# Second attention of a fused two-layer kernel: batch 1's high keys are copied by ScalarE instead of GpSimd, and three key pieces of batch 2 are split later

## The chip, the cores and the metric

The kernel is one program on 1 core of a Trainium2 chip. The metric is device time in microseconds (us) for one execution, the median of several. The engines are TensorE (PE; its weight loads are PEld), VectorE (DVE), ScalarE (ACT), GpSimd (POOL) and SyncE (SP), which issues most DMA transfers. Each engine runs its own instructions in order, and semaphores hold it back where it needs another engine's result.

## The reference, cut to what matters

Two layers of cross-attention and expert feed-forward are applied to `x` of shape 8 x 256 x 256 (batch, rows, features), with a context `ctx_2048` of 8 x 1601 x 256. The change touches the attention of the second layer, in which the context is key and value at once:

```python
def _L1_xattn_ref(hidden_states, memory_tokens, memory_mask):
    scores = jnp.einsum('bsd,bmd->bsm', hidden_states, memory_tokens) * scale      # scale = 256 ** -0.5
    scores = jnp.where(memory_mask[:, None, :], scores, neg_inf)
    attn = jax.nn.softmax(scores, axis=-1)
    readout = jnp.einsum('bsm,bmd->bsd', attn, memory_tokens)
    return jnp.where(valid_b[:, None, None], readout, 0)
...
x = x + _L0_xattn_ref(_layernorm(x), ctx_2048, ...)
x = x + _L0_ffn_ref(_layernorm(x), ...)
x = x + _L1_xattn_ref(_layernorm(x), ctx_2048, mask_BxS2_bk0)
x = x + _L1_ffn_ref(_layernorm(x), ...)
```

Everything is float32 in the reference. The kernel gets that accuracy from TensorE by splitting each operand into a high part (a copy rounded to the type `fp32r`) and a low part (original minus high), and adding three products: high x high, high x low, low x high.

## The kernel before

The program runs its stages one after the other: projections, the first attention (most of the time), the first feed-forward (`moe_two_of_eight`), the second attention (`memory_attention`), routing (`route_to_slots`) and the second feed-forward (`moe_slots`). `memory_attention` runs from 2519 us to about 2700 us of the span.

**Units.** `x` is 16 tiles of 128 rows, two to a batch. `memory_attention` works one tile at a time; a tile is a unit, and `body(i, last)` does four units u = 0 to 3, which are two batches, for i = 0 to 3. The 13 blocks of 128 keys of a batch are cut into four pieces, `MEM_PIECES`: pieces 0 to 2 have three blocks (128x768 elements, two features per partition and key) and piece 3 has four (128x1024). For a unit n and piece p:

- TensorE computes the scores into `ps_s` (`scores`, six matmuls in `score_piece`, L1426 to L1428); VectorE adds the mask's penalty and takes the piece's maximum (`piece_maximum`, L2215), then the row's (`negative_maximum`, L2222).
- ScalarE takes the exponential (`exp`, L2124); TensorE transposes the probabilities into `ps_t` (`transposes`, L2342); ScalarE copies them as high part (`high`, L2133) and VectorE subtracts for the low part (`low`, L2240).
- TensorE multiplies them with the context's rows (`products`, L2359 to L2361). VectorE forms the inverse of the row sum (`inverse_sum`, L2226 to L2231) and adds to `x` (`add_x`, L2248).

A later unit's normalised rows are made by GpSimd (`normalise`, L2074; VectorE's own for tiles 2 and 3, L2191), transposed (`transpose_x`, L2323), and split by `high_x` (ScalarE, L2139) and `low_x` (VectorE, L2198).

**Order of the work.** It is written out by hand, the same slots s = 0 to 3 on each engine. On TensorE slot s of unit u holds: the transposes of two pieces ahead, the products of piece s, in slot 2 `transpose_x` of unit u + 3, then the scores of unit u + 2, piece s. So the scores of unit 2, the first of batch 1, are made in the four slots of unit 0, and those of unit 4, the first of batch 2, in unit 2.

**Keys and rows.** The context is loaded twice for each batch, as transposed keys (`load_keys`, L1401) and as rows (`load_rows`, L1406), each into one raw buffer without a second copy (`area`, keys half and rows half). A piece of the next batch is loaded by SyncE once the present one has been split. For keys: `t_hi` (ScalarE, `split_t`, L2109) and `t_lo` (GpSimd, `split_t`, L2060); for rows: `r_hi` (ScalarE, `split_r`, L2116) and `r_lo` (GpSimd, `split_r`, L2068). The keys of even batches go to `keys_even`, those of odd ones to `keys_odd`. Batch 0's keys are split in the stage before. What is special at the start of this stage:

- Batch 1's high keys are four copies by GpSimd (L2079), its low keys four subtractions by VectorE (`low_t`, L2253): piece 0 ahead of unit 0, pieces 1 to 3 in slots 1 to 3 of unit 0. The scores of unit 2 wait for each (`wait_low`).
- Batch 0's rows: high parts by ScalarE (three ahead of the exponentials of unit 0, the fourth behind `high_x`); low parts 0 and 1 by VectorE (`low_r`, L2259), 2 and 3 by GpSimd.
- Batch 2's keys: high and low parts of piece 0 in slot 0 of unit 0, piece 1 in slot 2 of unit 0, pieces 2 and 3 in unit 1. Batch 1's rows lie between them, in the odd slots on ScalarE.

SyncE loads in the order batch 2's keys piece x, batch 1's rows piece x, for x = 0 to 3; each keys load waits for `low_t` of that piece.

## Time and profile before

| | |
|---|---|
| median of 3 runs | 2907.09 us (2905.89 to 2907.46) |
| the profiled execution | 2901.44 us |
| its span (first to last instruction) | 2899.6 us |
| busy share of the span: PE, PEld, DVE, ACT, POOL | 96%, 84%, 71%, 68%, 59% |
| mean granted TensorE clock | 0.979 of full speed |
| opening of the second attention, TensorE's first score of it to the first product of unit 0 | 2519.1 to 2529.1 us of the span |
| units 0, 1, 2, 3 by TensorE | 15.4, 10.8, 11.8, 10.8 us |

Times in the rows are microseconds from the span's start. A busy share says how long an engine worked, not whether anyone waited for it; for a change that moves a few instructions within 40 us, the rows of those 40 us count. A matmul's recorded duration contains its drain, so consecutive matmuls overlap and their pitch is shorter than their duration; other engines' instructions overlap by about 0.1 us in the same way. "[1.81 <-DVE pt_lo L2240]" behind a row says that the engine was idle for 1.81 us ahead of it and that VectorE's `pt_lo` ended the wait.

### The profile page before, as it was taken

Reading aid. Unit: us, or ns where it says so; the run is one execution under the profiler, and the core shown is the slowest. Engines: PE = TensorE matmul, PEld = TensorE weight load, DVE = VectorE, ACT = ScalarE, POOL = GpSimd, SP = SyncE. Lnnn points to the kernel's source line nnn. Section 1 sums busy time; section 2 is a strip of 40 time slices with the busy share of each in tenths; the row PEclk is TensorE's granted clock in tenths of the full one; section 3 lists DMA queues with packets and bytes.
Section 4 is the critical chain, followed back from the end, with each engine's and each line's share of the span. In section 5 each row is a group of like instructions: output and inputs, shape, how many; then the busy total and the mean of one; then the engine's idle time right before and its main releaser. Section 6 shows DMA issues by size and latency. Waiting matters only on the chain. (4 is left out here: it accounts for less than half of the span.)

```text
span 2899.6 us, 57707 instructions
## 1 busy us (share of the span) xinstructions
PE 2774.8 (96%) x18157; PEld 2441.3 (84%) x18157; DVE 2056.7 (71%) x4859; ACT 1968.1 (68%) x4913; POOL 1711.9 (59%) x2139
## 2 busy tenths in 40 slices
PE   7989999799999999999999999999999998799698
PEld 5768888699999999999999999999999985599655
DVE  7985445577777777777777777777777778965444
ACT  5656666577777777777777777777777756766111
POOL 6766663366665665666666566666656537587122
PEclk9999999899999999999999999999999998999699
DMA  5447667611111211111111111111111016364510
GB/s 184 133 143 217 205 206 209 211 43 71 50 50 44 70 57 43 71 53 47 46 68 57 43 71 56 44 48 66 57 43 71 15 37 145 80 198 132 191 36 27
DMA packets 284603, 263.46 MB, mean 91 GB/s; under 512 B 46382, under 2 KB 260527, under 8 KB 284304
## 3 DMA queue, kind: packets, MB, share of 16 engines
q1 hardware_dynamic: 264784, 238.94, 25.9%
q10 hardware_dynamic: 17312, 15.73, 1.9%
q0 software_dynamic: 2208, 5.12, 0.6%
q8 instruction: 148, 2.42, 0.4%
q14 instruction: 151, 1.24, 0.1%
HBM read 167.34 MB, written 84.93 MB: 87 GB/s over the span
## 5 line engine op out<-in xcount | busy, mean ns | idle before, releaser
L1031 ACT ACTIVATE w_hi<-ps_t 128x512 fp32r<-128x512 f32 (+2 forms) x1024 | 568.5, 555 | 352.6 <-PE ps_t L1274 344.3
L1133 DVE TENSOR_TENSOR w_lo<-ps_t,w_hi 128x512 fp32r<-128x512 f32 (+2 forms) x1024 | 655.8, 640 | 178.6 <-ACT w_hi L1031 175.3
L1107 DVE TENSOR_REDUCE piece_max<-ps_s 128x1 f32<-128x512 f32 (+1 forms) x768 | 472.3, 622 | 238.3 <-PE ps_s L1261 221.8
L1294 PE MATMUL ps_o<-w_hi,v_hi 128*128 128x256 f32 (+1 forms) x1856 | 596.0, 321 | 0.0
L1204 POOL TENSOR_SCALAR prob<-prob,inv_sum 128x512 f32<-128x512 f32 (+2 forms) x768 | 478.2, 642 | 189.6 <-DVE inv_sum L1123 189.6
L1296 PE MATMUL ps_o<-w_hi,v_lo 128*128 128x256 f32 (+1 forms) x1856 | 523.5, 282 | 0.0
L1295 PE MATMUL ps_o<-w_lo,v_hi 128*128 128x256 f32 (+1 forms) x1856 | 522.2, 281 | 0.0
L1274 PE MATMUL ps_t<-ident,prob 128*128 128x128 f32 (+1 forms) x2784 | 517.7, 273 | 0.0
L1274 PEld LDWEIGHTS ps_t<-ident,prob 128*128 128x128 f32 (+1 forms) x2784 | 357.1, 140 | 62.7 <-DVE w_lo L1133 8.7
L1259 PE MATMUL ps_s<-k_hi,q_hi 128*128 128x512 f32 (+2 forms) x1024 | 395.8, 387 | 10.2 <-PEq L58 4.8
L1260 PE MATMUL ps_s<-k_lo,q_hi 128*128 128x512 f32 (+2 forms) x1024 | 377.5, 369 | 0.0
L1261 PE MATMUL ps_s<-k_hi,q_lo 128*128 128x512 f32 (+2 forms) x1024 | 375.9, 367 | 0.0
L1019 ACT ACTIVATE prob<-ps_s,neg_max 128x512 f32<-128x512 f32 (+1 forms) x576 | 366.9, 637 | 0.0
L1295 PEld LDWEIGHTS ps_o<-w_lo,v_hi 128*128 128x128 f32 (+1 forms) x1856 | 353.7, 191 | 0.0
L1294 PEld LDWEIGHTS ps_o<-w_hi,v_hi 128*128 128x128 f32 (+1 forms) x1856 | 352.3, 190 | 0.0
L1296 PEld LDWEIGHTS ps_o<-w_hi,v_lo 128*128 128x128 f32 (+1 forms) x1856 | 350.0, 189 | 0.0
L1219 POOL TENSOR_TENSOR v_lo<-raw_v,v_hi 128x512 fp32r<-128x512 f32 x124 | 149.6, 1217 | 191.4 <-ACT v_hi L1047 191.4
L1274 PE MATMUL ps_t<-ident,first_prob 128*128 128x128 f32 (+1 forms) x928 | 230.1, 272 | 1.4 <-DVE w_lo L1133 1.2
L1212 POOL TENSOR_TENSOR k_lo<-raw_k,k_hi 128x480 fp32r<-128x480 f32 x124 | 148.9, 1222 | 138.8 <-ACT k_hi L1040 138.8
L1259 PEld LDWEIGHTS ps_s<-k_hi,q_hi 128*128 128x128 f32 x1024 | 194.9, 190 | 35.7 <-ACT prob L1019 18.2
L1261 PEld LDWEIGHTS ps_s<-k_hi,q_lo 128*128 128x128 f32 x1024 | 194.2, 190 | 28.1
L1260 PEld LDWEIGHTS ps_s<-k_lo,q_hi 128*128 128x128 f32 x1024 | 195.9, 191 | 2.9
(318 smaller groups left out, 6358.6 us busy)
## 6 DMA issues: line engine op xcount, KB each, us to landing
v_scratch<-v_out SPq DMA_DIRECT2D x120, 256.0 KB, 3.0
raw_k<-k_scratch SPq DMA_DIRECT2D x32, 960.0 KB, 7.0
raw_v<-v_scratch SPq DMA_DIRECT2D x32, 960.0 KB, 4.7
k_scratch<-k_out SPq DMA_DIRECT2D x104, 256.0 KB, 2.7
q_scratch<-out_t SPq DMA_DIRECT2D x64, 256.0 KB, 2.5
r_all<-r_scratch SPq DMA_DIRECT2D x32, 512.0 KB, 4.2
raw_q<-q_scratch SPq DMA_DIRECT2D x32, 512.0 KB, 5.1
first_prob<-in_ctx_t ACTq DMA_DIRECT2D x50, 256.0 KB, 2.8
```

What stands on the lines that cost most here:

```text
L1019: nc.scalar.activation(prob[n % PB][:, lo:hi], source, ACT.Exp, bias=neg_max[:, n % PB:n % PB + 1], accum_out=piece_sum[:, n % 2, p:p + 1] ...
L1031: nc.scalar.activation(pt_hi[keys, k % RING, cols], ps_t[keys, k % 2, cols], ACT.Copy).then_inc(hi_done, 1)
L1107: nc.vector.tensor_reduce(piece_max[:, n % 2, p:p + 1], ps_s[:, p, lo - p * PC:hi - p * PC], AX.X, ALU.max).then_inc(max_ready, 1)
L1133: nc.vector.tensor_tensor(pt_lo[keys, k % RING, cols], ps_t[keys, k % 2, cols], pt_hi[keys, k % RING, cols].bitcast(F32), ALU.subtract).th ...
L1204: nc.gpsimd.tensor_scalar(prob[n % PB][:, lo:hi], prob[n % PB][:, lo:hi], inv_sum[:, n % PB:n % PB + 1], 1.0, ALU.mult, ALU.mult).then_inc ...
L1259: nc.tensor.matmul(out, q_hi[gi][:, h, qs], k_hi[gi][:, lo:hi], start=True, stop=False)
L1260: nc.tensor.matmul(out, q_hi[gi][:, h, qs], k_lo[gi][:, lo:hi], start=False, stop=False)
L1261: nc.tensor.matmul(out, q_lo[gi][:, h, qs], k_hi[gi][:, lo:hi], start=False, stop=True).then_inc(scores_ready, 1)
L1274: last = nc.tensor.transpose(ps_t[0:keys, k % 2, at:at + P], prob[(2 * u + j) % PB][:, blk * P:blk * P + keys], ident[:, :])
L1294: nc.tensor.matmul(out, v_hi[gi][keys, vs], pt_hi[keys, k % RING, cols], start=blk == (0 if qt else 1), stop=False)
L1295: nc.tensor.matmul(out, v_hi[gi][keys, vs], pt_lo[keys, k % RING, cols], start=False, stop=False)
L1296: last = nc.tensor.matmul(out, v_lo[gi][keys, vs], pt_hi[keys, k % RING, cols], start=False, stop=blk == KB - 1)
```

## The change

In the opening, ScalarE copies batch 1's high keys (`first_t`), each behind the high part of the same piece of rows; GpSimd's four copies are gone. Two of batch 0's row pieces (1 and 2) are split after exponentials instead of ahead of them. In unit 0 only piece 0 of batch 2's keys is split; piece 1 is split at slot 0 of unit 1, piece 2 at slot 2 of unit 1, and piece 3 at slot 0 of unit 2, on ScalarE and on GpSimd. From there on the two programs are alike. The number of instructions on TensorE and VectorE and their order are the same.

```diff
--- before.py
+++ after.py
@@ -2074,9 +2074,6 @@
                     nc.gpsimd.tensor_scalar(xn[:, v % 2, :], x_sb[:, tile, :], mean_var[:, tile, 0:1], rstd_scaled[:, tile:tile + 1],
                                             ALU.subtract, ALU.mult).then_inc(xn_pool, 1)
 
-                for x in range(4):
-                    pool.wait_ge(t_loaded[x], 2 * 16)
-                    nc.gpsimd.tensor_copy(keys_of_piece(t_hi, 1, x), raw_of_piece(memory, x)).then_inc(th_first, 1)
                 for x in range(2, 4):
                     split_r(0, 0, x)
 
@@ -2088,8 +2085,15 @@
                             normalise(i, u + 4)
                         if i == 0 and u == 2:
                             norm_rstd(nc, pool, mean_var, rstd, half, norm, EARLY)
+                        if i == 0 and u == 2:
+                            split_t(0, 2, 3)
                         for x in (2 * (u % 2), 2 * (u % 2) + 1):
-                            if not last:
+                            if i == 0 and u < 2:
+                                if x == 0:
+                                    split_t(0, 2, 0)
+                                elif u == 1:
+                                    split_t(0, 2, x - 1)
+                            elif not last:
                                 split_t(i, u // 2 + 2, x)
                             if not (last and u >= 2):
                                 split_r(i, u // 2 + 1, x)
@@ -2145,16 +2149,25 @@
                     act.sem_inc(store_begun, 1)
                     act.dma_start(x_rows[bass.ds(at * P, P), :], x_sb[:, bass.ds(at, 1), :].rearrange("p a n -> p (a n)")).then_inc(rows_written, 16)
 
+                def first_t(x):
+                    act.wait_ge(t_loaded[x], 2 * 16)
+                    nc.scalar.activation(keys_of_piece(t_hi, 1, x), raw_of_piece(memory, x), ACT.Copy).then_inc(th_first, 1)
+
                 split_r(0, 0, 0)
+                first_t(0)
+                act.wait_ge(zeroed, 1)
+                exp(0, 0, 0)
+                exp(0, 0, 1)
                 split_r(0, 0, 1)
+                first_t(1)
+                high(0, 0, 0)
+                exp(0, 0, 2)
+                exp(0, 0, 3)
+                high_x(0, 2)
                 split_r(0, 0, 2)
-                act.wait_ge(zeroed, 1)
-                for p in range(SL):
-                    exp(0, 0, p)
-                    if p == 1:
-                        high(0, 0, 0)
-                high_x(0, 2)
+                first_t(2)
                 split_r(0, 0, 3)
+                first_t(3)
 
                 def body(i, last):
                     for u in range(UB):
@@ -2164,7 +2177,14 @@
                             if exists(u + 1, last):
                                 exp(i, u + 1, s)
                             x = 2 * (u % 2) + s // 2
-                            if s % 2 == 0 and not last:
+                            if i == 0 and u < 2:
+                                if s == 0 and u == 0:
+                                    split_t(0, 2, 0)
+                                elif s % 2 == 0 and u == 1:
+                                    split_t(0, 2, x - 1)
+                            elif s % 2 == 0 and not last:
+                                if i == 0 and u == 2 and s == 0:
+                                    split_t(0, 2, 3)
                                 split_t(i, u // 2 + 2, x)
                             if s % 2 == 1 and not (last and u >= 2):
                                 split_r(i, u // 2 + 1, x)
```

ScalarE at the opening of the second attention. `r_hi` is the high part of batch 0's rows, `keys_odd` batch 1's high keys, `prob` an exponential of unit 0, `pt_hi` the high part of transposed probabilities, `xt_hi` that of tile 2; `keys_even` is batch 2's piece 0. Before:

```order
L2116 ACTIVATE r_hi<-area 128x768 x3
L2124 ACTIVATE prob,piece_sum<-prob,neg_max 128x384 x2
L2133 ACTIVATE pt_hi<-ps_t 128x384
L2124 ACTIVATE prob,piece_sum<-prob,neg_max 128x384
L2124 ACTIVATE prob,piece_sum<-prob,neg_max 128x449
L2139 ACTIVATE xt_hi<-ps_o 128x256
L2116 ACTIVATE r_hi<-area 128x1024
L2133 ACTIVATE pt_hi<-ps_t 128x384
L2124 ACTIVATE prob,piece_sum<-prob,neg_max 128x384
L2109 ACTIVATE keys_even<-area 128x3x2x128
```

And now, from the first exponentials on (ahead of them stand one `r_hi` and one `keys_odd` of 128x768):

```order
L2128 ACTIVATE prob,piece_sum<-prob,neg_max 128x384 x2
L2120 ACTIVATE r_hi<-area 128x768
L2154 ACTIVATE keys_odd<-area 128x3x2x128
L2137 ACTIVATE pt_hi<-ps_t 128x384
L2128 ACTIVATE prob,piece_sum<-prob,neg_max 128x384
L2128 ACTIVATE prob,piece_sum<-prob,neg_max 128x449
L2143 ACTIVATE xt_hi<-ps_o 128x256
L2120 ACTIVATE r_hi<-area 128x768
L2154 ACTIVATE keys_odd<-area 128x3x2x128
L2120 ACTIVATE r_hi<-area 128x1024
L2154 ACTIVATE keys_odd<-area 128x4x2x128
L2137 ACTIVATE pt_hi<-ps_t 128x384
```

Between `xt_hi` of tile 2 and the second `pt_hi` there is one copy before, and there are four now.

GpSimd at the opening and through unit 0 (`r_lo` and `keys_even` low parts, `xn` a normalised tile). Before:

```order
L2054 MEMSET prob 128x2x63
L2079 CAST keys_odd<-area 128x3x2x128 x3
L2079 CAST keys_odd<-area 128x4x2x128
L2068 TENSOR_TENSOR r_lo<-area,r_hi 128x768
L2068 TENSOR_TENSOR r_lo<-area,r_hi 128x1024
L2074 TENSOR_SCALAR xn<-x_sb,mean_var,rstd 128x256
L2060 TENSOR_TENSOR keys_even<-area,keys_even 128x3x2x128
L2068 TENSOR_TENSOR r_lo<-area,r_hi 128x768
L2060 TENSOR_TENSOR keys_even<-area,keys_even 128x3x2x128
L2068 TENSOR_TENSOR r_lo<-area,r_hi 128x768
```

And now:

```order
L2068 TENSOR_TENSOR r_lo<-area,r_hi 128x768
L2068 TENSOR_TENSOR r_lo<-area,r_hi 128x1024
L2074 TENSOR_SCALAR xn<-x_sb,mean_var,rstd 128x256
L2060 TENSOR_TENSOR keys_even<-area,keys_even 128x3x2x128
L2068 TENSOR_TENSOR r_lo<-area,r_hi 128x768 x2
L2074 TENSOR_SCALAR xn<-x_sb,mean_var,rstd 128x256
L2060 TENSOR_TENSOR keys_even<-area,keys_even 128x3x2x128
```

The four copies are gone, and between batch 1's first two row pieces no piece of keys is split any more.

GpSimd around the start of unit 2, from batch 1's last row piece on. Before:

```order
L2068 TENSOR_TENSOR r_lo<-area,r_hi 128x1024
L2074 TENSOR_SCALAR xn<-x_sb,mean_var,rstd 128x256
L103 TENSOR_SCALAR norm_var_eps<-mean_var 128x4
L105 TENSOR_TENSOR rstd<-norm_var_eps,half 128x4
L2060 TENSOR_TENSOR keys_odd<-area,keys_odd 128x3x2x128
```

And now:

```order
L2068 TENSOR_TENSOR r_lo<-area,r_hi 128x1024
L2074 TENSOR_SCALAR xn<-x_sb,mean_var,rstd 128x256
L103 TENSOR_SCALAR norm_var_eps<-mean_var 128x4
L105 TENSOR_TENSOR rstd<-norm_var_eps,half 128x4
L2060 TENSOR_TENSOR keys_even<-area,keys_even 128x4x2x128
L2060 TENSOR_TENSOR keys_odd<-area,keys_odd 128x3x2x128
```

Batch 2's last and largest key piece stands ahead of batch 3's first.

## Rows read from the trace of the kernel before

**Rows 1.** Windows: units 0 to 3; us, busy time of each engine, clock, DMA share

```profile
2529.08:2544.53 15.45, 12.83 (x76) 11.88 (x76) 11.84 (x20) 7.36 (x17) 12.63 (x6) 0.89 0.38 123
2544.53:2555.31 10.78, 10.78 (x79) 10.43 (x78) 5.68 (x18) 7.92 (x17) 8.97 (x6) 1.00 1.04 331
2555.31:2567.14 11.83, 11.04 (x79) 10.38 (x78) 9.57 (x27) 7.50 (x17) 11.13 (x8) 1.00 0.48 123
2567.14:2577.96 10.82, 10.82 (x79) 10.46 (x78) 5.67 (x18) 7.92 (x17) 8.99 (x6) 1.00 0.76 237
```

**Rows 2.** Waits of PE, 2518 to 2700 us: total, times, longest

```profile
PE ps_t L2342 <- DVE pt_lo L2240: 2.7, 3, 1.8
PE ps_s L1426 <- DVE keys_odd L2253: 2.6, 3, 1.2
...
PE ps_o L2359 <- DVE xt_lo L2198: 1.0, 1, 1.0
```

**Rows 3.** Windows, the stretch of unit 0 with a low clock; columns as in rows 1

```profile
2530.10:2533.40 3.30, 3.30 (x15) 3.20 (x14) 3.12 (x7) 1.91 (x6) 3.30 (x3) 0.50 0.01 3
```

**Rows 4.** Timeline of VectorE: start, duration, instruction

```profile
2521.74 1.79 DVE L2259 TENSOR_TENSOR r_lo<-area,r_hi 128x768 fp32r<-128x768 f32 x1
2523.45 2.59 DVE L2253 TENSOR_TENSOR keys_odd<-area,keys_odd 128x768 fp32r<-128x768 f32 x1
...
2529.41 2.33 DVE L2259 TENSOR_TENSOR r_lo<-area,r_hi 128x768 fp32r<-128x768 f32 x1
...
2533.55 1.29 DVE L2231 SCALAR_TENSOR_TENSOR inv_sum<-neg_max,inv_row 128x1 f32<-128x1 f32 x1
2534.76 0.94 DVE L2253 TENSOR_TENSOR keys_odd<-area,keys_odd 128x768 fp32r<-128x768 f32 x1
...
2541.92 1.21 DVE L2253 TENSOR_TENSOR keys_odd<-area,keys_odd 128x1024 fp32r<-128x1024 f32 x1
...
2559.72 1.57 DVE L2231 SCALAR_TENSOR_TENSOR inv_sum<-neg_max,inv_row 128x1 f32<-128x1 f32 x1
```

**Rows 5.** Timeline of GpSimd

```profile
2519.24 3.48 POOL L2079 CAST keys_odd<-area 128x768 fp32r<-128x768 f32 x4
2522.69 2.54 POOL L2068 TENSOR_TENSOR r_lo<-area,r_hi 128x768 fp32r<-128x768 f32 x1
2528.54 2.39 POOL L2068 TENSOR_TENSOR r_lo<-area,r_hi 128x1024 fp32r<-128x1024 f32 x1 [3.31 <-ACT r_hi L2116]
2530.91 2.10 POOL L2074 TENSOR_SCALAR xn<-x_sb,mean_var,rstd 128x256 f32<-128x256 f32 x1
2532.99 1.83 POOL L2060 TENSOR_TENSOR keys_even<-area,keys_even 128x768 fp32r<-128x768 f32 x1
2534.78 2.61 POOL L2068 TENSOR_TENSOR r_lo<-area,r_hi 128x768 fp32r<-128x768 f32 x1
...
2542.07 2.77 POOL L2068 TENSOR_TENSOR r_lo<-area,r_hi 128x768 fp32r<-128x768 f32 x1 [0.19 <-ACT r_hi L2116]
2544.83 1.22 POOL L2074 TENSOR_SCALAR xn<-x_sb,mean_var,rstd 128x256 f32<-128x256 f32 x1
...
2559.41 1.86 POOL L2060 TENSOR_TENSOR keys_odd<-area,keys_odd 128x768 fp32r<-128x768 f32 x1
```

**Rows 6.** Timeline of ScalarE

```profile
2519.11 2.32 ACT L2116 ACTIVATE r_hi<-area 128x768 fp32r<-128x768 f32 x3 [4.10 <-PEq L58]
...
2527.41 1.05 ACT L2116 ACTIVATE r_hi<-area 128x1024 fp32r<-128x1024 f32 x1
2528.36 0.48 ACT L2133 ACTIVATE pt_hi<-ps_t 128x384 fp32r<-128x384 f32 x1
...
2539.11 0.84 ACT L2109 ACTIVATE keys_even<-area 128x768 fp32r<-128x768 f32 x1 [4.52 <-DMA area<-in_ctx_t]
```

**Rows 7.** Timeline of SyncE's queue: batch 1's rows, piece 1

```profile
2536.25 0.44 SPq L1406 DMA_DIRECT2D area<-in_ctx  x1
```

**Rows 8.** DMA issues, 2535 to 2545 us: count, KB each, median us to landing

```profile
area<-in_ctx SPq DMA_DIRECT2D x2, 384.0 KB, 3.7
```

## The prediction

> **What bounds the kernel now.** I read the windows of each unit first, then TensorE's waits, then the timelines of the other engines over the opening and unit 0. The windows [rows 1] show TensorE busy for all of units 1 and 3 (10.78 of 10.78 us, 10.82 of 10.82): there nothing of this change can help. Unit 0 takes 15.45 us for nearly the same matmuls, unit 2 takes 11.83. In unit 0 and its opening TensorE waits for VectorE: for `pt_lo` and `xt_lo` ahead of the first product, and three times (2.6 us) for the low keys of batch 1 [rows 2]. From 2530.1 to 2533.4 the granted clock is half, 1.2 instead of 2.4 GHz, after TensorE had stood nearly idle [rows 3]. So the most that could be won is small: unit 0's excess of 4.7 us over unit 1, and the waits of 1.8 and 1.0 us ahead of it [rows 1, 2], 7.5 us in all.
>
> The chain that sets unit 0's length is: a low key piece on VectorE, the scores on TensorE, the maximum on VectorE, the next low key piece. Its head is low key piece 1, done at 2534.76 + 0.94 = 2535.70 [rows 4]. What holds the head back? The small `inv_sum` ahead of it took 1.29 us; it ends at 2534.84, just as GpSimd's `keys_even` low part ends (2532.99 + 1.83 = 2534.82) [rows 4, 5]. The same holds of every VectorE instruction with two operands in SBUF in these rows. The low rows at 2521.74 took 1.79 us and the low keys at 2523.45 took 2.59, where 0.94 is the duration without company; GpSimd's `r_lo` of 2.61 us behind the low keys of 2534.76 paid the same way [rows 4, 5]. One waits for the other's end.
>
> So the head of the chain is timed by GpSimd: `r_lo` piece 3 from 2528.54 to 2530.93, then VectorE's low rows 1, which had waited and end at 2531.74 (2529.41 + 2.33), then `xn` to 2533.01, then `keys_even` to 2534.82 [rows 4, 5].
>
> **Part 1: the opening, +1.55 us.** Removed are four copies, 3.48 us of GpSimd [rows 5]. With them go VectorE's two waits: 1.79 - 0.94 = 0.85 us, and 2.59 - 0.94 = 1.65 us [rows 4]. VectorE reaches the maxima of unit 1 earlier, and the first products, which had waited 1.0 us for `xt_lo` [rows 2], start about 1.0 us earlier. That is not on the chain above, since GpSimd times its head.
>
> Added are four copies on ScalarE. A 128x768 copy has a pitch of 0.74 (three of them 2.32, of which the last is 0.83) and a 128x1024 one of 0.95 (2527.41 to 2528.36) [rows 6]. The first two fall into ScalarE's free time before the first transposes are there, and cost nothing; without that cover they would cost 1.5. Behind `high_x`, which still starts its successor at 2527.41, there stood one copy (0.95), and now stand `r_hi` 2, `keys_odd` 2, `r_hi` 3, `keys_odd` 3: 0.74 + 0.74 + 0.95 + 0.95 = 3.4 us. The second `pt_hi` moves from 2528.36 to 2530.8 [rows 6], and VectorE, in order, can do its low part and then low rows 1 only from 2531.7.
>
> GpSimd is hit harder. It did `r_lo` piece 2 at 2522.69, in time nobody else wanted; now ScalarE has that piece's high part only at 2527.41 + 0.83 = 2528.24. So: `r_lo` 2 to 2528.24 + 1.83 = 2530.07, and `r_lo` 3, whose high part is done by 2529.95, to 2530.07 + 2.39 = 2532.46, where it was 2530.93: 1.53 later. Low rows 1 on VectorE, `xn`, `keys_even` and `inv_sum` follow as before, and low key piece 1 ends at 2537.25 for 2535.70. **+1.55**, which I take. From below the bound is 0, if something else lets VectorE run ahead. From above it is 1.55 + 1.83: behind `inv_sum` both engines want to go, GpSimd waited and VectorE won [rows 4, 5]; if GpSimd wins, its `r_lo` of 1.83 comes first.
>
> **Part 2: batch 2's keys piece 1 leaves unit 0, +0.75 us.** Before, ScalarE stopped 4.52 us for that load [rows 6], and `high_x`, `pt_hi` and an exponential stood behind the wait. The wait goes. By itself it earns nothing: the chain's next maximum had to wait for its scores anyhow. What comes next is earlier on GpSimd: `r_lo` of batch 1's piece 1 started at 2542.07, 0.15 behind VectorE's low key piece 3 (2541.92), and so paid for it (2.77) [rows 4, 5]. Now that its `r_hi` isn't held up, it is timed by its own load: issued at 2536.25 [rows 7], 1.55 later now, 2537.80, plus 3.7 to land [rows 8] is 2541.5, plus 0.84 for the copy is 2542.35. `r_lo` runs from 2542.4 to 2544.2. Low key piece 3 wants to start at 2541.92 + 1.55 = 2543.47 and waits till 2544.2. **+0.75.** The bounds are 0 (the load lands over 1 us later, and VectorE is first as before) and 1.8 (a whole `r_lo`).
>
> Unit 0 ends 2.3 us later. Unit 1 has neither idle nor extra work on TensorE, so it passes this on whole. The split of pieces 1 and 2 there takes the place of pieces 2 and 3 on both engines; it adds nothing, and the cover is ScalarE's 2.9 idle us and GpSimd's 1.8 [rows 1].
>
> **Part 3: unit 2, +0.55 us.** `inv_sum` waited 1.57 us there, until the `keys_odd` piece of 1.86 ended (2559.41 to 2561.27) [rows 4, 5]. In that place now stands the four-block piece, 2.39 by the `r_lo` of that size [rows 5]: 0.53 longer. `add_x` behind it lets TensorE transpose the next tile, and TensorE had no reserve of more than the parts of a microsecond that unit 2 still idles (11.83 - 11.04) [rows 1]. I take **+0.55**; the bounds are 0 and 0.95, the copy that ScalarE does in addition. After that GpSimd has 2.4 us more to do, against about 1.8 idle in a unit like 3 [rows 1]; batch 3's keys are due only in unit 4, so I cost the rest at nothing. If it were not covered, it would be up to 0.6 us.
>
> **Sum:** 1.55 + 0.75 + 0.55 = 2.85 us, less nothing that counts. Of the profiled execution that is 2901.44 to 2904.3. The median of the runs lies 5.65 us above the profiled one, and I add the change to the median: 2907.09 + 2.8 = **2909.9 us**. That is 0.1%. About 0.2% (5.8 us) is what a measurement can tell from no change, so the call is "no change", on its slow side.
>
> **Rivals.**
> 1. *The waits that go are time won: -2.5 us, 2904.6.* For it: VectorE was busy or waiting through nearly the whole opening, and 0.85 + 1.65 us of its time go [rows 4]. Against it: low rows 1 and low keys 1 are timed by GpSimd's own chain, which starts later. The Trainium skill, "SBUF — State Buffer", section "two separate sides", says the pair of ports shared by VectorE and GpSimd is an exclusive lock held for a whole instruction, while ScalarE has its own. By that rule the move to ScalarE takes the waits away; the trace agrees (2.59 beside GpSimd, 0.94 alone), and that speaks for this rival as far as it goes. Chance 0.11.
> 2. *All hidden, 0 us, 2907.1.* VectorE gets ahead and the new waits are shorter than I sum. The change would have moved slack alone. Chance 0.13.
> 3. *GpSimd wins behind `inv_sum`: +1.8 more, 2911.7.* Chance 0.11, since before VectorE won in the same constellation.
> 4. *Slower beyond what can be told: the clock, 2913.9.* TensorE has more idle time between 2530 and 2541 than before. If the half clock of rows 3 does not end before the scores on the chain but holds from 2533 through unit 0 and into unit 1, each of three score pieces on the chain takes twice its time, about 0.8 us more (six matmuls at unit 1's mean of 10.78 / 79 = 0.14 [rows 1]), 2.4 in all, and unit 1 loses half of another 3.3 us, 1.6: 2.8 + 4.0 = +6.8. It decides if the low stretch lasts over 10 us; against it stands that it lasted 3.3 before. Chance 0.08.
> 5. *Faster by over 5.8 us.* It would need most of the 7.5 us above, or a shift elsewhere in the program. Chance 0.03.
>
> My forecast has the rest, 0.54, with a range of its own from +1.5 to +4.5 us. The range 2904.5 to 2913.5 takes in the forecast, rivals 1 to 3 and the spread of the runs shown (1.6 us); it leaves out rivals 4 and 5 and some scatter. Faster by over 0.2%: 0.03. Slower by over 0.2%: 0.08 and a little of rival 3's upper end, 0.10. Within 0.2%: 0.87.
>
> **What would show it.** In the changed profile: no wait in VectorE's first low rows and low keys (0.94 each). First products about 1 us earlier, at 2528.1. ScalarE's second `pt_hi` at 2530.8. GpSimd's `r_lo` 2 at 2528.2, and low key piece 1 ending at 2537.2. No wait of ScalarE for keys in unit 0. Low key piece 3 at about 2.0 us instead of 1.21, because `r_lo` stands before it. Unit 1 ending at 2557.6 for 2555.3. In unit 2 an `inv_sum` of 2.1. I am wrong if low key piece 1 ends before 2536, or if unit 0 ends before 2545.5, or if the clock is low at another place for over 3.3 us.

## The result

The changed kernel takes 2910.95 us (median of 20 runs, 2907.02 to 2914.53), the kernel before 2906.09 us (20 runs, 2904.73 to 2909.50). The ratio is 1.0016, with a 95% interval from 1.0010 to 1.0022: 4.9 us slower, some 3 to 6 us by the interval. The forecast was 2909.9 us in a range of 2904.5 to 2913.5. The profiled execution has a span of 2905.2 us for 2899.6.

The program as a whole is a coarse measure for this. The second attention's first scores by TensorE begin at 2519.1 us in both profiles shown here, but at 2519.2 to 2529.1 in those of the experiments, whose stages ahead of it are alike. So in what follows I measure the **stage**: from the start of its first score matmul to the start of its last `add_x` on VectorE. Before it is 2697.59 - 2519.13 = 178.46 us, now 2701.93 - 2519.07 = 182.86 us: **4.4 us longer**. The last 1.2 us between the spans lie behind the stage, and the code there is the same; over all fourteen profiles that rest varies between 202.0 and 203.5 us. Right behind the stage the granted clock is half for 54.6 us in the profile before and for 58.0 us in the changed one, and the four profiles with 58.0 us have the four longest rests (203.2 to 203.5 us). That the clock makes these 1.2 us is likely by this, not shown.

Windows of the changed kernel, units 0 to 2 and the stretch of low clock (columns as in [rows 1]):

```profile
2528.15:2548.12 19.97, 13.96 (x75) 12.43 (x76) 12.57 (x20) 9.80 (x21) 14.64 (x7) 0.83 0.26 81
2548.12:2558.90 10.78, 10.78 (x80) 10.43 (x78) 5.68 (x18) 7.71 (x17) 6.87 (x4) 1.00 0.95 288
2558.90:2571.27 12.37, 11.03 (x79) 10.39 (x78) 9.30 (x27) 8.45 (x18) 11.67 (x8) 1.00 0.48 156
2533.70:2540.10 6.40, 4.67 (x19) 4.28 (x19) 4.44 (x9) 1.61 (x4) 5.19 (x3) 0.50 0.23 73
```

Unit 0 grew from 15.45 to 19.97 us, of which 0.93 are an earlier start; unit 1 passes it on to the hundredth; unit 2 adds 0.5 to 0.6; unit 3, not shown, takes 0.15 more than its 10.81. The low clock [rows 3] now lasts about 6.8 us instead of 3.4 (the window shown lies inside it), and it lies later.

TensorE's waits, 2518 to 2700 us, for [rows 2]:

```profile
PE ps_s L1426 <- DVE keys_odd L2273: 3.9, 3, 1.7
PE ps_t L2362 <- ACT prob L2128: 2.3, 2, 1.4
...
PE ps_o L2379 <- DVE r_lo L2279: 0.8, 1, 0.8
```

The timeline of VectorE, for [rows 4]:

```profile
2521.68 0.95 DVE L2279 TENSOR_TENSOR r_lo<-area,r_hi 128x768 fp32r<-128x768 f32 x1
2522.55 0.95 DVE L2273 TENSOR_TENSOR keys_odd<-area,keys_odd 128x768 fp32r<-128x768 f32 x1
...
2531.23 0.56 DVE L2260 TENSOR_TENSOR pt_lo<-ps_t,pt_hi 128x384 fp32r<-128x384 f32 x1 [3.13 <-ACT pt_hi L2137]
2531.70 1.56 DVE L2279 TENSOR_TENSOR r_lo<-area,r_hi 128x768 fp32r<-128x768 f32 x1
...
2534.82 1.51 DVE L2251 SCALAR_TENSOR_TENSOR inv_sum<-neg_max,inv_row 128x1 f32<-128x1 f32 x1
2536.26 0.94 DVE L2273 TENSOR_TENSOR keys_odd<-area,keys_odd 128x768 fp32r<-128x768 f32 x1
...
2539.69 0.56 DVE L2235 CUSTOM_DVE_ANT_0 prob<-ps_s,pen 128x384 f32<-128x384 f32 x1 [1.89 <-PE ps_s L1428]
...
2541.08 0.95 DVE L2273 TENSOR_TENSOR keys_odd<-area,keys_odd 128x768 fp32r<-128x768 f32 x1
...
2544.39 2.35 DVE L2273 TENSOR_TENSOR keys_odd<-area,keys_odd 128x1024 fp32r<-128x1024 f32 x1
...
2564.19 1.23 DVE L2251 SCALAR_TENSOR_TENSOR inv_sum<-neg_max,inv_row 128x1 f32<-128x1 f32 x1
```

The two waits of the opening are gone (0.95 each), and in their place VectorE stands idle for 3.13 us until the second `pt_hi` comes. Low key piece 1 ends at 2537.20. Its scores run under the half clock, so their maximum comes late, and the last low key piece takes 2.35 us. GpSimd, for [rows 5]:

```profile
2528.27 4.18 POOL L2068 TENSOR_TENSOR r_lo<-area,r_hi 128x768 fp32r<-128x768 f32 x2 [9.03 <-ACT r_hi L2120]
2532.43 2.09 POOL L2074 TENSOR_SCALAR xn<-x_sb,mean_var,rstd 128x256 f32<-128x256 f32 x1
2534.51 1.80 POOL L2060 TENSOR_TENSOR keys_even<-area,keys_even 128x768 fp32r<-128x768 f32 x1
2536.28 2.61 POOL L2068 TENSOR_TENSOR r_lo<-area,r_hi 128x768 fp32r<-128x768 f32 x1
2543.82 1.83 POOL L2068 TENSOR_TENSOR r_lo<-area,r_hi 128x768 fp32r<-128x768 f32 x1 [4.93 <-ACT r_hi L2120]
```

It idles 9.03 us in the opening, and `r_lo` of batch 1's piece 1 (2543.82 to 2545.65) lies right across VectorE's last low key piece. ScalarE, for [rows 6]:

```profile
2529.77 1.05 ACT L2154 ACTIVATE keys_odd<-area 128x1024 fp32r<-128x1024 f32 x1
2530.72 0.48 ACT L2137 ACTIVATE pt_hi<-ps_t 128x384 fp32r<-128x384 f32 x1
...
2541.60 0.38 ACT L2143 ACTIVATE xt_hi<-ps_o 128x256 fp32r<-128x256 f32 x1 [6.29 <-PE ps_o L2343]
```

It no longer waits for a load of keys. It now waits at the same place, and for longer (6.29 for 4.52 us), for TensorE's transposes of the next tile. Batch 1's rows piece 1, issued at 2537.75, had landed at 2541.57; ScalarE came to its high part only at 2542.90.

### The profile page after: what moved, and what is told of

It is laid out like the page before. It is cut to its first block and busy times, and to the rows that moved or that the text cites. A ratio compares the mean times of both kernels' runs of the same rounds, so it can differ in the third digit from the quotient of the medians.

```text
span 2905.2 us, 57707 instructions
## 1 busy us (share of the span) xinstructions
PE 2777.9 (96%) x18157; PEld 2441.5 (84%) x18157; DVE 2054.5 (71%) x4859; ACT 1971.1 (68%) x4917; POOL 1707.0 (59%) x2135
## 5 line engine op out<-in xcount | busy, mean ns | idle before, releaser
L1259 PEld LDWEIGHTS ps_s<-k_hi,q_hi 128*128 128x128 f32 x1024 | 194.8, 190 | 35.8 <-ACT prob L1019 18.2
```

The lines of the kernel that those rows point to most:

```text
L1259: nc.tensor.matmul(out, q_hi[gi][:, h, qs], k_hi[gi][:, lo:hi], start=True, stop=False)
```

## The experiments

Twelve runs, of eleven kernels, stood beside the kernel before, with 7 to 12 executions each. Times in this table are counted from the stage's first score matmul, in us, and come from one profile of each run; the ratio comes from all its executions. "Low key piece 1" is where the chain begins; "half clock" is where the clock falls and rises, up to the middle of unit 1.

| kernel | second pt_hi | low key piece 1 ends | piece 2 starts | piece 3: start, duration | unit 1 begins | stage | half clock | ratio to before, interval |
|---|---|---|---|---|---|---|---|---|
| before | 9.2 | 16.57 | 19.48 | 22.79, 1.21 | 25.40 | 178.46 | 11.0 to 14.4 | 1 |
| changed | 11.65 | 18.13 | 22.01 | 25.32, 2.35 | 29.05 | 182.86 | 14.4 to 21.2 | 1.0016 [1.0010, 1.0022] |
| e1_copies | 11.65 | 18.12 | 22.00 | 25.29, 2.80 | 29.87 | 184.46 | 15.3 to 22.2, 29.0 to 32.4 | 1.0015 [1.0007, 1.0024] |
| e2_late | 9.2 | 16.57 | 19.48 | 22.76, 2.02 | 26.18 | 180.01 | 10.8 to 14.2 | 1.0003 [0.9995, 1.0012] |
| e3_rows_first | 11.65 | 18.09 | 21.89 | 25.17, 2.63 | 29.77 | 185.15 | 18.2 to 21.7, 28.5 to 31.9 | 1.0014 [1.0005, 1.0023] |
| e4_yield | 11.66 | 18.15 | 22.02 | 25.60, 1.22 | 28.19 | 182.06 | 9.9 to 13.3, 16.7 to 23.5 | 1.0011 [1.0002, 1.0020] |
| e5_rows3 | 9.97 | 16.39 | 20.27 | 24.03, 2.85 | 28.27 | 181.41 | 15.4 to 22.3 | 1.0003 [0.9994, 1.0011] |
| e6_filler | 11.64 | 18.13 | 27.05 | 30.33, 1.98 | 33.71 | 187.56 | none | 1.0026 [1.0017, 1.0035] |
| e7_filler_before | 9.2 | 18.31 | 28.09 | 31.38, 1.98 | 34.76 | 187.92 | none | 1.0031 [1.0020, 1.0042] |
| e11_filler_light | 11.65 | 18.14 | 21.05 | 24.34, 2.15 | 27.87 | 181.76 | none | 1.0015 [1.0006, 1.0024] |
| e10_spread | 8.28 | 13.69 | 16.60 | 19.98, 1.22 | 22.60 | 175.68 | none | 0.9988 [0.9979, 0.9997] |
| e12_spread_inv | 8.29 | 13.71 | 16.61 | 20.03, 1.21 | 22.62 | 175.53 | none | 0.9994 [0.9985, 1.0003] |
| e13_spread_late | 8.28 | 13.69 | 16.60 | 19.89, 2.21 | 23.49 | 177.28 | none | 0.9998 [0.9988, 1.0007] |
| e14_spread_again | 8.29 | 13.72 | 16.62 | 19.91, 1.22 | 22.51 | 175.63 | none | 0.9993 [0.9984, 1.0002] |

### Each part alone

`e1_copies` is the changed kernel with batch 2's pieces split where they were:

```diff
-                            if i == 0 and u < 2:
-                                if s == 0 and u == 0:
-                                    split_t(0, 2, 0)
...
-                            elif s % 2 == 0 and not last:
-                                if i == 0 and u == 2 and s == 0:
-                                    split_t(0, 2, 3)
+                            if s % 2 == 0 and not last:
                                 split_t(i, u // 2 + 2, x)
```

(ScalarE's loop; the same in GpSimd's.)

> Only the first part: ScalarE makes batch 1's high key copies, batch 2's pieces are split where they were. My theory: the head of the chain (VectorE's low key piece 1) ends about 1.5 us later than before (2537.2 for 2535.7), because GpSimd's r_lo pieces 2 and 3 start late. ScalarE's stop for batch 2's keys is back (4 to 6 us), so GpSimd's next r_lo is late again and low key piece 3 has its short duration of 1.2 us; unit 2's inv_sum is at about 1.6 us, not more. Time against the kernel before: +1.6 us with the clock full on the chain, up to +3.5 if the half clock lies on its scores. Rival (the deferral is what costs, the copies are hidden): 0, with low key piece 1 at 2535.7.

Low key piece 1 ends at 18.12, 1.55 later than before, as the sum had it. The rest of the expectation missed: low key piece 3 has not its short duration but the longest of all, 2.80. ScalarE's stop for the load is back (5.33 us), and yet GpSimd's `r_lo` was first, by 0.11 us:

```profile
2549.12 1.82 POOL L2068 TENSOR_TENSOR r_lo<-area,r_hi 128x768 fp32r<-128x768 f32 x1 [0.53 <-ACT r_hi L2113]
```

```profile
2549.23 2.80 DVE L2259 TENSOR_TENSOR keys_odd<-area,keys_odd 128x1024 fp32r<-128x1024 f32 x1
```

The half clock had delayed VectorE's side of the race by 1 us (piece 2 starts 3.88 us behind the end of piece 1, where it was 2.91 before), and a second fall of the clock made unit 1 longer. So the copies alone make the stage 6.0 us longer. Of that, 1.55 are the opening and 1.6 are the wait of low key piece 3. The other 2.8 are 1.0 on the scores of piece 1 under the half clock, 0.4 from low key piece 3 to the start of unit 1, and 1.5 in unit 1, where the clock is half for 2.5 us and `inv_sum` waits, too (1.63 us for 0.22).

The two parts of the change don't add up: with the copies in one heap, the later split makes the stage 1.6 us shorter (182.86 for 184.46), because GpSimd's `r_lo` is further ahead (low key piece 3 2.35 for 2.80) and the clock doesn't fall a second time. In the program's time (1.0015 and 1.0016) that doesn't show.

`e2_late` is the kernel before with only the later split (the lines above, the other way round).

> Only the second part: GpSimd keeps the copies, batch 2's three key pieces are split later. My theory: the opening is as before (low key piece 1 ends at 2535.7), low key piece 3 takes up to 2.4 us instead of 1.2 because r_lo now stands before it, unit 2's inv_sum waits longer than 1.57 by the four-block piece. Time against the kernel before: +1.2 us (0.65 + 0.55). Rival (the copies alone cost): 0. Second rival (ScalarE's 4.5 us stop was worth something): -0.5 to -1.

Stage +1.55 us, unit 0 +0.78, which is low key piece 3 (2.02 for 1.21). The opening is as before to the hundredth. The rest, 0.77, comes behind unit 0: unit 2's `inv_sum` ends at 43.51 for 42.16 from the first score, 1.35 later, of which 0.78 was there already; unit 3 adds 0.15. For the whole program that can't be told from no change. It was worth nothing that ScalarE no longer stopped: low key piece 3 starts at 22.76 for 22.79. VectorE and GpSimd of this run at low key piece 3:

```profile
2542.45 2.02 DVE L2267 TENSOR_TENSOR keys_odd<-area,keys_odd 128x1024 fp32r<-128x1024 f32 x1
```

```profile
2541.55 1.85 POOL L2068 TENSOR_TENSOR r_lo<-area,r_hi 128x768 fp32r<-128x768 f32 x1 [3.60 <-PE ps_s L1428]
```

### What times the head of the chain

`e3_rows_first` is the changed kernel with ScalarE's row copies ahead of its key copies:

```diff
                 exp(0, 0, 1)
                 split_r(0, 0, 1)
-                first_t(1)
+                split_r(0, 0, 2)
                 high(0, 0, 0)
                 exp(0, 0, 2)
                 exp(0, 0, 3)
                 high_x(0, 2)
-                split_r(0, 0, 2)
-                first_t(2)
                 split_r(0, 0, 3)
+                first_t(1)
+                first_t(2)
                 first_t(3)
```

> The changed kernel, but ScalarE splits batch 0's row pieces 1 and 2 ahead of the second exponentials' successors and piece 3 right behind high_x, and three of the key copies follow. The second pt_hi stays as late as in the changed kernel (2530.7). My theory (GpSimd's r_lo times the head): r_lo 2 runs early again, r_lo 3 ends at 2530.9, low key piece 1 ends at 2535.7 as before; unit 0 ends about 0.7 us later than before, all in all +1.2 us against the kernel before. Rival (the late pt_hi on ScalarE times the head): low key piece 1 stays at 2537.2 and the time is that of the changed kernel.

The rival's number came, against my own explanation. GpSimd is on time again: `r_lo` 3 ends at 2533.98 - 2522.18 = 11.80 from the first score, exactly where it ended before. The head is as late as in the changed kernel all the same (18.09). VectorE shows why:

```profile
2534.34 0.56 DVE L2260 TENSOR_TENSOR pt_lo<-ps_t,pt_hi 128x384 fp32r<-128x384 f32 x1 [3.13 <-ACT pt_hi L2137]
2534.82 0.95 DVE L2279 TENSOR_TENSOR r_lo<-area,r_hi 128x768 fp32r<-128x768 f32 x1
2535.68 2.03 DVE L2211 TENSOR_SCALAR xn<-x_sb,mean_var,rstd 128x256 f32<-128x256 f32 x1
```

```profile
2535.73 1.84 POOL L2060 TENSOR_TENSOR keys_even<-area,keys_even 128x768 fp32r<-128x768 f32 x1 [0.52 <-ACT keys_even L2113]
```

The late second `pt_hi` holds VectorE for 3.13 us. The low rows then have no wait. But VectorE's `xn` now meets GpSimd's `keys_even` and takes 2.03 us instead of 0.40: it ends only with GpSimd's instruction. GpSimd in turn had idled 0.52 us for the high part of `keys_even`, which stands on ScalarE behind the late `pt_hi`. So ScalarE's late queue is enough for the 1.5 us, with GpSimd's low rows on time, but only through this meeting. Without the 1.63 us of `xn`'s wait VectorE would have reached `inv_sum` at 15.1 and low key piece 1 would have ended near 16.3 (my estimate from these rows), no later than before. Whether a late `r_lo` alone would be enough too was not tried. The stage is 2.3 us longer than the changed kernel's: low key piece 3 takes 2.63, and the clock falls again in unit 1.

`e5_rows3` has batch 2's pieces split where they were, and this opening (against the changed kernel):

```diff
                 split_r(0, 0, 0)
                 first_t(0)
+                split_r(0, 0, 1)
                 act.wait_ge(zeroed, 1)
                 exp(0, 0, 0)
                 exp(0, 0, 1)
-                split_r(0, 0, 1)
+                split_r(0, 0, 2)
+                split_r(0, 0, 3)
                 first_t(1)
...
                 high_x(0, 2)
-                split_r(0, 0, 2)
                 first_t(2)
-                split_r(0, 0, 3)
                 first_t(3)
```

> As the run that copies on ScalarE alone, but row pieces 1, 2 and 3 come ahead of the first pt_hi, key piece 1 with them, and only key pieces 2 and 3 behind high_x, which is 1.7 us of copies there instead of 3.4 (0.95 before the change). My theory: second pt_hi at 9.9 to 10, low key piece 1 ends near 14.7, stage about 2 us shorter than before, some of it open to the half clock. Rival (GpSimd and the loads time the head whatever ScalarE does): low key piece 1 at 16.6 or later.

The second `pt_hi` came at 9.97 as foreseen, the head at 16.39 and not at 14.7: `xn` on VectorE started 0.04 us ahead of GpSimd's `keys_even` and waited for it, 2.02 us, as in `e3_rows_first`:

```profile
2540.95 2.02 DVE L2197 TENSOR_SCALAR xn<-x_sb,mean_var,rstd 128x256 f32<-128x256 f32 x1
```

```profile
2540.99 1.84 POOL L2060 TENSOR_TENSOR keys_even<-area,keys_even 128x768 fp32r<-128x768 f32 x1 [1.87 <-ACT keys_even L2106]
```

That is close to the rival's number (16.6 or later), but for this reason: GpSimd's low rows were long done, and it idled 1.87 us for ScalarE's high part of `keys_even`. Then the half clock took its part, and low key piece 3 waited for `r_lo` (2.85). The stage is 3.0 us longer than before, the program's ratio only 1.0003; the profiled execution was the slowest of its twelve (2915.32 us for a median of 2905.84), so its stage may not be the usual one.

### Who goes first on the last low key piece

`e4_yield` adds one wait to the changed kernel:

```diff
                             if not (last and u >= 2):
+                                if i == 0 and u == 0 and x == 1:
+                                    pool.wait_ge(tl_first, CT + 4)
                                 split_r(i, u // 2 + 1, x)
```

> The changed kernel, plus a wait: GpSimd starts r_lo of batch 1's row piece 1 only when VectorE has done its low key piece 3. My theory (the two engines exclude each other): low key piece 3 takes 1.2 us instead of 2.35, unit 0 ends 1.1 us earlier than in the changed kernel, and so does the program (-1.1). Rival (the duration of 2.35 has another cause, such as the loads landing): it stays above 2, and nothing is won.

The piece takes 1.22 us, and GpSimd's `r_lo` follows it:

```profile
2546.13 1.22 DVE L2275 TENSOR_TENSOR keys_odd<-area,keys_odd 128x1024 fp32r<-128x1024 f32 x1
```

```profile
2547.42 1.83 POOL L2068 TENSOR_TENSOR r_lo<-area,r_hi 128x768 fp32r<-128x768 f32 x1 [7.06 <-DVE keys_odd L2275]
```

Unit 1 begins 0.86 us earlier, the stage is 0.80 shorter; the rest of the 1.1 went to a later start of the piece (25.60 for 25.32) under a half clock that lasted until 23.5. That the two engines exclude each other here is shown: in the code nothing but GpSimd's turn was changed, and the wait is gone.

### The clock

`e6_filler` adds matmuls that keep TensorE busy while it waits, into score banks that the next scores overwrite:

```diff
+                def filler(n, p):
+                    pe.wait_ge(max_ready, SL + p + 1)
+                    for _ in range(n):
+                        nc.tensor.matmul(ps_s[:, p, 0:P], ident[:, :], ident[:, :], start=True, stop=True)
```

It is called with 8 and 12 ahead of the first products, 12 behind the scores of piece 0, 6 and 24 around the second products.

> The changed kernel with 62 additional matmuls (ident by ident, 128 columns, into score banks that are free, overwritten later) in TensorE's waits of the opening and unit 0. My theory (the half clock follows TensorE's idle stretches, and costs 1 us on the chain): the granted clock stays at 2.4 GHz over unit 0, low key piece 2 starts about 1 us earlier than 22.0 from the stage's first score, the stage is about 1 us shorter than the changed kernel's 182.9. Rival (the clock falls there for a reason of its own): the half clock stays, and the fillers at half speed make the stage 1 us longer or more.

The granted clock is 1.00 in every microsecond of unit 0. But the fillers were too long: 62 of them, at about 0.22 us each (each shows as two records, 0.11 us apart), made the stage 4.7 us longer. The run speaks for idle time as what brings the clock down, and says nothing on what that costs. `e7_filler_before` puts the same lines into the kernel before.

> The kernel before with the same 62 additional matmuls. My theory: the half clock between 11 and 14.3 from the stage's first score goes, but it hardly lay on the chain, so the stage is within 0.5 us of the 178.5 before, and spreads less from run to run. Rival (the half clock is a matter of the whole program): it stays or moves, and the time is 0.5 to 2 us longer for the fillers.

The clock stays full there too, and the stage is 9.5 us longer, for the most part for the same reason: the expectation that nothing would be lost was wrong. One part is another meeting. The fillers brought VectorE to its `inv_sum` 1.3 us late, and GpSimd's `r_lo` was first, by 0.05 us:

```profile
2539.51 1.78 DVE L2231 SCALAR_TENSOR_TENSOR inv_sum<-neg_max,inv_row 128x1 f32<-128x1 f32 x1
```

```profile
2539.46 1.81 POOL L2068 TENSOR_TENSOR r_lo<-area,r_hi 128x768 fp32r<-128x768 f32 x1
```

Low key piece 1 ends at 18.31 for 16.57. Hence a lighter dose, `e11_filler_light`: 3, 4, 5, 3 and 10.

> The changed kernel with 25 additional matmuls in TensorE's waits instead of 62, since one took about 0.22 us in the run before and 62 of them were longer than the waits. My theory (idle TensorE brings the half clock, and it costs 1 us on the chain and some more in the slower runs): clock full over unit 0, low key piece 2 starts at 21.0 to 21.3 from the stage's first score for 22.0, stage 181.9 or a little less for 182.9. Rival (the clock's fall costs nothing, VectorE waits anyhow): low key piece 2 stays at 22.0.

This is the clean one. Window over unit 0 of this run:

```profile
2533.00:2550.00 17.00, 13.90 (x102) 12.82 (x102) 12.34 (x20) 8.92 (x19) 13.28 (x7) 1.00 0.28 93
```

Low key piece 1 ends at 18.14 as in the changed kernel, piece 2 starts at 21.05 instead of 22.01, the stage is 181.76 instead of 182.86. By these two profiles the half clock costs the changed kernel 1.0 us on the chain and 1.1 of the stage. Additional work on TensorE made the stage shorter. In the program's time (1.0015) that doesn't show. Low key piece 3 still meets `r_lo`:

```profile
2547.26 2.15 DVE L2273 TENSOR_TENSOR keys_odd<-area,keys_odd 128x1024 fp32r<-128x1024 f32 x1
```

```profile
2546.49 1.84 POOL L2068 TENSOR_TENSOR r_lo<-area,r_hi 128x768 fp32r<-128x768 f32 x1 [3.72 <-ACT r_hi L2120]
```

### A version that beats both

`e10_spread` keeps the copies on ScalarE, but not in one heap. Against the kernel before:

```diff
                 split_r(0, 0, 0)
+                first_t(0)
                 split_r(0, 0, 1)
-                split_r(0, 0, 2)
                 act.wait_ge(zeroed, 1)
...
+                exp(0, 0, 0)
+                exp(0, 0, 1)
+                split_r(0, 0, 2)
+                split_r(0, 0, 3)
+                high(0, 0, 0)
+                exp(0, 0, 2)
+                exp(0, 0, 3)
                 high_x(0, 2)
-                split_r(0, 0, 3)
...
                                 exp(i, u + 1, s)
+                            if i == 0 and u == 0 and s < 3:
+                                first_t(s + 1)
```

and GpSimd's four copies are gone.

> ScalarE keeps the high key copies, but they don't stand ahead of the second pt_hi: row pieces 1 to 3 are split in its gaps of the opening, key piece 0 at the start, key pieces 1, 2 and 3 in slots 0, 1 and 2 of unit 0, where it used to stand still for a load. Batch 2's key pieces are split where they were before the change. Times from the stage's first score. My theory (the copies are cheap, their place behind high_x is what makes VectorE and GpSimd meet): second pt_hi at about 8.3 (9.2 before, 11.7 in the changed kernel), low key piece 1 ends near 13.7 instead of 16.6 and 18.1, stage 2 to 3 us shorter than before the change. Rival (any copy on ScalarE in this stretch costs its length): no shorter than before. The half clock can take 1 to 2 us of it back.

Every number came as expected: second `pt_hi` at 8.28, low key piece 1 at 13.69, stage 175.68, which is 2.8 us below the kernel before and 7.2 below the changed one. VectorE and GpSimd of this run:

```profile
2532.18 0.95 DVE L2264 TENSOR_TENSOR r_lo<-area,r_hi 128x768 fp32r<-128x768 f32 x1
2533.05 0.41 DVE L2196 TENSOR_SCALAR xn<-x_sb,mean_var,rstd 128x256 f32<-128x256 f32 x1
...
2535.40 0.21 DVE L2236 SCALAR_TENSOR_TENSOR inv_sum<-neg_max,inv_row 128x1 f32<-128x1 f32 x1
2535.53 0.94 DVE L2258 TENSOR_TENSOR keys_odd<-area,keys_odd 128x768 fp32r<-128x768 f32 x1
```

```profile
2527.38 4.15 POOL L2068 TENSOR_TENSOR r_lo<-area,r_hi 128x768 fp32r<-128x768 f32 x2 [4.44 <-ACT r_hi L2113]
2531.52 1.23 POOL L2074 TENSOR_SCALAR xn<-x_sb,mean_var,rstd 128x256 f32<-128x256 f32 x1
2533.74 1.84 POOL L2060 TENSOR_TENSOR keys_even<-area,keys_even 128x768 fp32r<-128x768 f32 x1 [1.00 <-ACT keys_even L2106]
```

`inv_sum` hardly waits (0.21), because both meetings fall away: VectorE's `xn` is done before GpSimd's `keys_even` starts (10.68 and 10.97 from the first score), and `keys_even` ends (12.81) as `inv_sum` comes (12.62). The clock stays full, without fillers. The program's ratio is 0.9988; one of its runs took 3952.92 us, which I can't explain and which is not in the ratio. Repeated as `e14_spread_again`:

> The spread copies a second time, unchanged, beside its variant and the kernel before on one chip. My theory: stage 175.7, the program 2 to 3 us below the kernel before (ratio 0.999). Rival (the first run's 0.9988 was luck of the chip): ratio 1.000 within its interval, though the stage is shorter.

Stage 175.63, ratio 0.9993, whose interval just reaches 1. The stage is 2.8 us shorter in both profiles; in the time of the program it is at the edge of what can be told, with 3.1 and 2.4 us between the medians.

`e12_spread_inv` adds `pool.wait_ge(inv_ready, 3)` behind GpSimd's `norm_rstd` in unit 2.

> The spread copies, and in unit 2 GpSimd waits for that unit's inv_sum before it starts on batch 3's keys. My theory: inv_sum there takes 0.2 instead of 1.56, the tile behind it is transposed about 0.2 to 0.4 us earlier, stage 0.2 to 0.4 us shorter than 175.7. Rival (the wait only moves GpSimd's work to where it is missed): as long or longer. The difference is too small for the program's time to show; the stage's length shows it.

`inv_sum` there takes 0.16 instead of 1.56, and the stage is 0.15 us shorter, less than the 0.2 to 0.4 expected. The unit itself shows the gain: from the first transpose of unit 2 to that of unit 3 it takes 11.56 us for 11.86 and, in the repeat, 11.84. What the stage keeps of these 0.3 us lies between 0.10 (against the repeat) and 0.15, while the two profiles of the unchanged kernel differ by 0.05, so that is barely told.

`e13_spread_late` adds the later split to the spread copies.

> The spread copies together with the change's second part, the later split of batch 2's key pieces 1 to 3. My theory: the later split costs here as it did alone (low key piece 3 meets r_lo: 1.9 to 2.4 us for 1.22; unit 2's inv_sum and the extra piece), stage 176.9 for the 175.7 of the spread copies, still below 178.5. Rival (with the copies out of the way the later split wins what it was made for, ScalarE's stop of 1.8 us): stage 175 or less.

Stage 177.28, 1.6 more where 1.2 were expected, with low key piece 3 at 2.21 us. The later split costs the same 1.6 us beside the spread copies as without them (1.55 in `e2_late`).

## Why the prediction was right, and where it wasn't

**Direction and size.** "No change, on its slow side" was right: the ratio's middle lies below 0.2%, its upper end just above. The sum was 2.85 us, and the stage grew by 4.4. By the runs: copies 1.56, clock 1.0, low key piece 3 1.14, unit 2 0.57, unit 3 0.15. The program's 4.9 us lie above the +1.5 to +4.5 that the forecast gave itself, the stage's 4.4 just inside. That 2910.95 comes within 1.1 us of 2909.9 is in part luck: the 20 runs put the kernel before at 2906.09, 1.0 us below the three runs from which the forecast started. And one sign that I had named for being wrong did come: the clock is low at another place for 6.8 us, which is over 3.3.

**The opening (+1.55).** The number was exact: low key piece 1 at 2537.20, where the prediction had 2537.25; the second `pt_hi` at 2530.72, `r_lo` 2 at 2528.27, first products at 2528.15. The trace follows the path of the prediction, from GpSimd's late `r_lo` to `keys_even` and `inv_sum`. But as a reason it was half of it. I wrote "GpSimd is hit harder" and costed the late `r_lo`. `e3_rows_first` gave GpSimd its time back and won nothing. In the changed kernel VectorE waits for both in turn; ScalarE's late queue by itself (`pt_hi`, and behind it the high part of `keys_even`) costs as much, by bringing VectorE's `xn` and GpSimd's `keys_even` together. The prediction had no such meeting, since it counted `xn` among the instructions that don't wait.

**The last low key piece (+0.75).** That `r_lo` would stand before it was right, and `e4_yield` shows it by turning it off. The size was low: 1.14. I had VectorE want the piece at 2543.47, 1.1 us behind the start of GpSimd's `r_lo` (2542.4 to 2544.2). Measured, VectorE came at 2544.39 and GpSimd ran from 2543.82 to 2545.65, so VectorE came only 0.57 us behind and waited longer (2.35 - 1.21 = 1.14). The chain was late by the clock. `r_lo` was late, too, though not by its own load, which the prediction took for its timer: that had landed at 2541.57, as summed (2541.5). Its `r_hi` stood on ScalarE behind `high_x`, a `pt_hi` and an exponential, and these had waited for TensorE's transposes until 2541.60, so that it started at 2542.90. The wait is there without the fall of the clock too: 2.15 in `e11_filler_light`, +0.94.

**Unit 2 (+0.55).** The end of `inv_sum` came 0.54 us later, as summed, and the unit is 0.57 us longer. Its duration, for which I had named 2.1 as the sign, was 1.23: ScalarE's additional copy made it start late, and GpSimd's longer piece made it end late, so the two overlap instead of adding. A late start hides in a wait.

**Cost at nothing.** Unit 1 did pass everything on. Unit 3 did not quite: it takes 0.15 us more, and its `inv_sum` 0.74 us for 0.21, because GpSimd is behind with batch 3's keys:

```profile
2575.66 0.74 DVE L2251 SCALAR_TENSOR_TENSOR inv_sum<-neg_max,inv_row 128x1 f32<-128x1 f32 x1
```

```profile
2574.55 1.84 POOL L2060 TENSOR_TENSOR keys_odd<-area,keys_odd 128x768 fp32r<-128x768 f32 x1
```

That is within the 0.6 that I had named for it.

**Rivals.** The clock (4) was put at 0.08 as a heavy case of 4 us. A lighter form of it happened: low for about 6.8 us instead of 3.4, on one score piece of the chain instead of three, 1.0 us. This is the step that failed: the sum held no term for the clock, although the prediction says itself that TensorE would idle more. It should have had one, with 0 to 1 us for each score piece on the chain.

The gain of 2.5 us by the exclusive ports (1) did not come from this change. The rule behind it, an exclusive lock by the Trainium skill's "SBUF — State Buffer", section "two separate sides", agrees with most of the meetings: VectorE's waits in the opening went (0.95 each). It does not agree with all of them. In `e10_spread` VectorE's `r_lo` (2532.18, two operands in SBUF) started 0.66 us behind GpSimd's `xn` (2531.52 to 2532.75), the two overlapped by 0.56 us, and neither took longer than alone (0.95 and 1.23); `e3_rows_first`, `e12_spread_inv`, `e13_spread_late` and `e14_spread_again` show the same. There the measurement decides. `e10_spread` also shows the gain of 2.8 us that was there once the copies stood elsewhere.

GpSimd did not win behind `inv_sum` (3) in any of the runs. But it can get in ahead of it: in `e7_filler_before` its `r_lo` did by 0.05 us, and the head came 1.7 us later, about the rival's price. In `e3_rows_first` and `e5_rows3` `r_lo` went ahead of `inv_sum` as well, since `xn` had held VectorE back. That rival 3's +4.65 us (2911.7) lies nearer to the result than the forecast does is chance, since what it priced did not happen in the changed kernel.

**The spread.** The changed kernel's runs lie in 7.5 us, those of the kernel before in 4.8. The half clock fell at a different place in nearly each profile of the slower kernels, and in `e1_copies` and `e3_rows_first` it fell twice. That this makes a wider spread is not shown, nor is the wider spread itself: beside the experiments the kernel before lies in 5.6 to 10.8 us (20 to 35 runs each), and `e11_filler_light`, whose profile has a full clock over unit 0, in 9.7.

## What to carry to other kernels

When work moves to an engine that has idle time, ask what stands behind it in that engine's queue, not only whether it fits: 3.4 us of copies in front of one instruction cost 1.6 us and more, and copies of the same pieces in the gaps of the same engine gained 2.8. Where two engines exclude each other, price a change by who arrives first at each meeting, and keep a way to choose (a semaphore wait) in hand; 0.1 us decided over 1.6 us, and in one run 0.05 over 1.7. And give each added idle stretch of TensorE a term for the clock.

## What the runs showed of the hardware

- TensorE's granted clock fell from 2.4 to 1.2 GHz in stretches of about 3.4 or 6.8 us, in the middle of a stage in which it is over 90% busy (171.98 of 178.46 us before). Ahead of the fall it had waited 1.81 and 0.95 us in the kernel before, and 0.94, 0.95, 1.39 and 0.76 us in the changed kernel; in `e10_spread`, with waits of 0.94, 0.95, 0.79 and 0.93 us, it did not fall. Twenty-five small matmuls in its waits kept it at 2.4 GHz through the whole of unit 0, and the stage was 1.1 us shorter; sixty-two made it 4.7 us longer.
- A VectorE `tensor_scalar` with one tensor operand (128x256 float32, in SBUF) can wait for GpSimd like the ones with two: 2.03 and 2.02 us instead of 0.40 in two runs, each time ending with GpSimd's `keys_even` (a `tensor_tensor`), and each time started 0.04 to 0.05 us ahead of it. I had counted only instructions with two operands. Beside GpSimd's own `xn` it took 0.40 (2531.66 before, 2533.18 changed).
- Starts that lie so close don't tell who goes first. In `e14_spread_again` VectorE's low key piece 3 has its start 0.01 us behind GpSimd's `r_lo`, and it was GpSimd that paid:

```profile
2543.48 1.22 DVE L2258 TENSOR_TENSOR keys_odd<-area,keys_odd 128x1024 fp32r<-128x1024 f32 x1
```

```profile
2543.47 2.92 POOL L2068 TENSOR_TENSOR r_lo<-area,r_hi 128x768 fp32r<-128x768 f32 x1 [0.18 <-ACT r_hi L2113]
```

- Where VectorE follows its own `inv_sum` with another such instruction, it kept GpSimd out in the changed kernel as in the kernel before (GpSimd's `r_lo` 2.61 us both times).
